# Causal attention prologue: another order of the features, of the stores and of the second batch's projections

## The chip, the cores and the metric

One core of one Trainium2 chip runs the whole program. The metric is the device time of one execution in microseconds; the kernel before took 1536.09 us, the median of three runs (1533.88 to 1536.41).

## What is computed

The program is a two-layer decoder on x of shape (2, 1024, 256), float32. Each step is added to x: linear attention with a feed-forward part, cross attention to a context of 64 rows, a recurrence, then in the second layer causal attention, context attention and a mixture of experts. The change is in the second layer's causal attention:

```python
h = layernorm(x)                            # (2, 1024, 256)
q, k, v = split(h @ Wqkv + bqkv)            # 16 heads of 16 features
score = einsum('bhsd,bhtd->bhst', q, k)     # keys after the query are masked out
attn = softmax(score / sqrt(16))
x = x + einsum('bhst,bhtd->bhsd', attn, v).reshape(2, 1024, 256) @ Wout + bout
```

## The kernel before

Everything is kept transposed, features on partitions and tokens on the free axis. Five engines run programs of their own, written out by hand and held together by semaphores; SP issues all DMAs. The layer is `causal_attention_layer`, L1761 to L2401.

**Three-part products.** q and k are float32, but their products are made in bfloat16: each of the two is split into three bfloat16 parts (the value, the rest, the rest of the rest), and six products of parts are stacked on the contraction axis. A stack is six times 16 rows, so 96 partitions; `Q_PART` and `K_PART` (L3641) say which part stands in which of the six places. Two more rows carry the negated maximum of each query, the "shift", against rows of ones in the key stack. Four heads (a "quad") lie side by side on the free axis: a stack is 98 partitions x 4 heads x 1024 tokens. There are four quads in a batch and two batches, so eight stacks of q and eight of k, kept in three buffers.

**How a stack is made.** ACT copies the projections of a batch out of PSUM with the bias (L2216) and casts parts 0 and 1 (L2235); DVE makes the rests and part 2 (L2291, L2293). Head h, feature d lies on row h*16+d. SP stores each part, 256 rows of 1024 tokens, to DRAM (`store`, L1926) in one DMA of 128 partitions and 512 KB, and loads it back in another shape (`load_part`, L1907): 16 partitions, the features, each with the four heads' rows of 2 KB one after the other. That is 12 DMAs of 128 KB for a quad: six for part 0, four for part 1, two for part 2. For the first batch SP's order is: store q0, k0, q1; wait for the part 0 stores; load part 0 of quad 0; store k1, q2, k2; wait for the part 1 stores, load part 1; wait for the part 2 stores, load part 2; then the second quad's 12 loads; then the first shift's rows (`keep_shift`, L1930) and the third quad's loads.

**What PE does meanwhile.** For batch 0 it projects q, k and v, then for batch 1 all of q, all of k and two of four groups of v (L2037 to L2059). Then come the first pieces. A "piece" is one PSUM tile of scores, query on the partition, made only to take its maximum per query on DVE (`reduce`, L2300). The first half of a quad's queries has eleven pieces (`NPC_0`). When they are reduced, DVE makes the negated maximum in two bfloat16 parts (`split_shift`, L2307, its operations at L2317 and L2319), PE transposes it (`turn_shift`, L2081), DVE copies it (L2326), SP moves its rows into the query stack (L1934), and only then PE can make the real scores (`scores`, L2088), ACT their exponentials (L2255), POOL the diagonal mask (L1998) and PE the values (`values`, L2104). The last two groups of v of batch 1 stand between the first pieces (L2161 to L2167). From there on PE alternates scores, pieces of later halves and values as `count_pieces` says.

**What POOL does meanwhile.** After its constants it waits until all six stores of the first batch have landed (L1977), because it writes the second batch's parts over the same tensors: a cast and a subtraction for each part, four operations for q and four for k (L1982 to L1988), and a memset of ones (L1991). Then it begins with the masks.

Of the kernel before, what the change touches and what calls it, by code (L numbers as in the profile page):

```python
# [28 lines left out]
P = 128  # L29
B, S, D = 2, 1024, 256  # L30
# [1730 lines left out]
def causal_attention_layer(nc, c):  # L1761

    H, DH = 16, 16
# [3 lines left out]
    HALVES = 2 * STEPS  # L1767
    ROWS, SHIFT = len(Q_PART) * DH, 2
    LOADS = 2 * len(Q_PART) * 16
    PAD = 32  # L1770
    RING = 16
    SCORES, TILES = 3, 4
# [56 lines left out]
    upto = count_pieces()  # L1829
# [18 lines left out]
    with ExitStack() as ctx:  # L1848
        bn, yn = c.bn, c.yn
        pr = c.signals(nc, "bp", dict(q_proj=4, k_proj=4, v_proj=4, q_raw=4, k_raw=4, v_copied=4))  # L1850
        s = c.signals(nc, "b", dict(part=0, rest=0, last_part=0, stored0=0, stored1=0, stored2=0, later_part=0, later_stored=0, ones=0, masks=0, k_ones=0,
                                       loaded0=0, loaded1=0, loaded2=0, shifted0=0, shifted1=0, made=0, read=0,
                                       max_step=0, parts=0, scored=0, expd=0, masked=0, av=0, out_copied=0, inv=0))
        set_round(0, s, pr)
# [47 lines left out]
        with nc.Block() as block:  # L1902

            @block.sync
            def _(sync):
                def load_part(n, i):

                    b, quad = divmod(n, QUADS)
                    a = n % 3
                    by_head = lambda ap: ap.rearrange("(h d) n -> d h n", d=DH)  # L1910
                    rows = slice(quad * QUAD * DH, (quad + 1) * QUAD * DH)
                    for r in range(len(Q_PART)):
                        if Q_PART[r] == i:
                            sync.dma_start(qs[a][r * DH:(r + 1) * DH], by_head(q_dram[b, i, rows, :])).then_inc(loaded[a].sem, 16)
                        if K_PART[r] == i:
                            sync.dma_start(ks[a][r * DH:(r + 1) * DH], by_head(k_dram[b, i, rows, :])).then_inc(loaded[a].sem, 16)

                def loads(n):
                    if n == 2:
                        sync.wait_ge(*pr["v_proj"](8))  # L1920
                    if n >= 3:
                        sync.wait_ge(*s["scored"](tiles_upto(first_group(2 * (n - 2)) - 1)))
                    for i in range(3):
                        load_part(n, i)

                def store(b, n, i, done):  # L1926
                    dram, parts = ((q_dram, q_parts), (k_dram, k_parts))[n]
                    sync.dma_start(dram[b, i].rearrange("(m p) n -> p m n", p=P), parts[:, i, :, :]).then_inc(done.sem, 16)

                def keep_shift(hs):  # L1930
                    _, _, half = part_of(hs)
                    sync.wait_ge(*s["read"](nth["shift", hs] + 1))
                    for i in range(SHIFT):
                        sync.dma_start(qs[hs // 2 % 3][ROWS + i:ROWS + i + 1, :, half * CH:(half + 1) * CH],  # L1934
                                       stage[i * QUAD:(i + 1) * QUAD, hs % 2, :]).then_inc(shifted[hs % 2].sem, 16)

                for n in range(2):
                    sync.wait_ge(*s["part"](n + 1))
                    store(0, n, 0, stored[0])
                sync.wait_ge(*s["part"](3))  # L1940
                store(0, 0, 1, stored[1])
                sync.wait_ge(*stored[0](2 * 16))
                load_part(0, 0)
                sync.wait_ge(*s["part"](4))
                store(0, 1, 1, stored[1])
                for n in range(2):
                    sync.wait_ge(*s["last_part"](n + 1))
                    store(0, n, 2, stored[2])
                for i in (1, 2):
                    sync.wait_ge(*stored[i](2 * 16))  # L1950
                    load_part(0, i)
                loads(1)
                keep_shift(0)
                loads(2)
                for hs in range(1, HALVES):
                    keep_shift(hs)
                    if hs == 3:
                        for n in range(2):
                            sync.wait_ge(*s["later_part"](4 * (n + 1)))
                            for i in range(3):  # L1960
                                store(1, n, i, s["later_stored"])
                    if hs % 2 == 1 and 3 <= hs // 2 + 2 < STEPS:
                        if hs // 2 + 2 == QUADS:
                            sync.wait_ge(*s["later_stored"](6 * 16))
                        loads(hs // 2 + 2)

            @block.gpsimd
            def _(pool):
# [7 lines left out]
                pool.memset(k_stack[ROWS:ROWS + SHIFT, :, :, :], 1.0).then_inc(s["k_ones"].sem)  # L1976
                for done in stored:  # L1977
                    pool.wait_ge(*done(2 * 16))
                pool.wait_ge(*s["k_ones"](1))
                for n, (raw, parts, ready) in enumerate(((raw_of[1][0], q_parts, pr["q_raw"]), (raw_of[1][1], k_parts, pr["k_raw"]))):  # L1980
                    pool.wait_ge(*ready(8))
# [35 lines left out]
            def _(pe):  # L2017
# [34 lines left out]
                for n in range(4):  # L2052
                    pe.wait_ge(*pr["k_raw"](n + 1))
                    project_in(1, "b_wq", n, c.bank(4 + n), pr["q_proj"])
                for n in range(4):
                    pe.wait_ge(*pr["v_copied"](n + 1))
                    project_in(1, "b_wk", n, c.bank(n), pr["k_proj"])
                later_value(0)
                later_value(1)  # L2059

                def tile(what):
                    n = nth[what]
# [41 lines left out]
                def values(pair):  # L2104
                    hs, first_ki = groups[2 * pair]
                    b, quad, half = part_of(hs)
                    pe.wait_ge(*s["expd"](tiles_upto(2 * pair + 1)))
                    if first_ki >= 4 * half:
                        pe.wait_ge(*s["masked"](diagonal_upto(2 * pair + 1)))
                    if first_ki == 0 and hs >= 1:  # L2110
                        pe.wait_ge(*s["out_copied"](hs))
                    for i in range(2):
                        ki, n = first_ki + i, width(first_ki + i, half)
                        for h in range(QUAD):
                            mm = pe.matmul(out_tile[h * PAD:(h + 1) * PAD, CH - n:CH], v_aug[:, b * TT + ki, quad * QUAD + h, :],  # L2115
                                           probs[(QUAD * (2 * pair + i) + h) % RING][:, 0:n],
                                           start=(ki == 0), stop=(ki == 4 * half + 3))
                    mm.then_inc(s["av"].sem)
# [36 lines left out]
                def more_pieces(first, last):  # L2155
                    for p in range(first, last):
                        piece(p)
                        if turned_after(p) is not None:
                            turn_shift(turned_after(p))

                pe.wait_ge(*s["masks"](2))  # L2161
                pe.wait_ge(*pr["q_raw"](8))
                more_pieces(0, 4)
                later_value(2)
                more_pieces(4, 8)
                later_value(3)
                more_pieces(8, upto[0])  # L2167
                pe.wait_ge(*s["k_ones"](1))
                pe.wait_ge(*pr["v_copied"](8))
                for slot in range(QUAD * len(groups)):  # L2170
                    (hs, ki), x = groups[slot // QUAD], slot % QUAD
                    if (slot // QUAD, x) in tile_at:
# [1594 lines left out]
```

## Time and profile before

| | us |
|---|---|
| median of three runs | 1536.09 |
| lowest, highest | 1533.88, 1536.41 |
| profiled execution | 1545.4 |
| its span | 1543.6 |
| PE busy | 1452.9 |
| DVE busy | 986.8 |
| ACT busy | 753.1 |
| POOL busy | 494.0 |

All times inside the program are counted from the start of the profiled execution's span. PE, DVE, ACT and POOL are the engines' busy times; SP is the engine that issues DMAs. The profiled execution is one run of its own; its 1545.4 us are 1.8 above its span and 9.3 above the median. The causal layer's projections begin at about 637 us, the first piece at 683.64, the first scores at 699.90.

### The profile page before, as it was taken

To read this page: it belongs to the slowest core of one execution; us is meant where nothing else is said; L and a number is where in the kernel's file an instruction comes from. 1 tells how busy PE (TensorE), PEld (TensorE's weight loads), DVE (VectorE), ACT (ScalarE), POOL (GpSimd) and SP (SyncE) were. 2 spreads that over 40 slices of the span, in tenths; PEclk is the share of its full clock that TensorE was granted. 3 is DMA by queue.
4 is the path that set the end of the run, shared out by engine and by line. 5 is a ranking of instruction groups with operands and counts; after the bars stand their busy time and mean duration, and the time that the engine had idled before them with its cause. 6 is when DMAs were issued, how large, how long until landed. Compare 5 with 4: busy or idle time off the path is not lost. (4 is left out here: it accounts for less than half of the span.)

```text
span 1543.6 us, 19029 instructions
## 1 busy us (share of the span) xinstructions
PE 1452.9 (94%) x6910; PEld 848.3 (55%) x6914; DVE 986.8 (64%) x1506; ACT 753.1 (49%) x1237; POOL 494.0 (32%) x410
## 2 busy tenths in 40 slices
PE   6999999989999999888999998898889999999998
PEld 3757764432232265453444443322568888888886
DVE  5774243768877743548888783676677575664853
ACT  5466344443334451543666565434655545445442
POOL 0046420123132410343111112102136655655562
PEclk9999997999999999998999999899999999999999
DMA  7000000000000000083535300000313223223201
GB/s 293 1 0 0 1 1 4 0 1 1 0 1 1 1 0 0 1 164 42 125 51 74 42 3 1 4 1 4 133 42 110 69 83 100 78 74 104 73 10 55
DMA packets 39044, 67.55 MB, mean 44 GB/s; under 512 B 3944, under 2 KB 19368, under 8 KB 38568
## 3 DMA queue, kind: packets, MB, share of 16 engines
q1 hardware_dynamic: 38952, 66.33, 16.1%
q8 instruction: 56, 0.92, 0.3%
q14 instruction: 36, 0.29, 0.1%
HBM read 57.80 MB, written 8.39 MB: 43 GB/s over the span
## 5 line engine op out<-in xcount | busy, mean ns | idle before, releaser
L2255 ACT ACTIVATE arena<-psum 128x512 f32<-128x512 f32 (+1 forms) x304 | 155.2, 583 | 109.9 <-PE psum L2100 109.2
L2303 DVE TENSOR_REDUCE b_mx<-psum 128x1 f32<-128x512 f32 (+3 forms) x304 | 179.6, 650 | 45.0 <-PE psum L2078 36.9
L3047 POOL TENSOR_TENSOR m_w_rest<-m_w,m_w_high 128x512 fp32r<-128x512 f32 (+1 forms) x88 | 111.6, 1270 | 155.6 <-ACT m_w_high L3246 155.6
L3497 DVE TENSOR_TENSOR m_hidden<-m_gelu,psum 128x512 f32<-128x512 f32 (+1 forms) x88 | 60.4, 686 | 148.6 <-ACT m_gelu L3338 124.4
L3140 PE MATMUL psum<-m_x_high,m_w_high 128*128 128x512 f32 (+1 forms) x352 | 138.4, 393 | 3.2 <-issue 3.2
L3053 POOL TENSOR_TENSOR m_h_rest<-m_hidden,m_h_high 128x512 fp32r<-128x512 f32 (+1 forms) x88 | 122.4, 1390 | 58.9 <-ACT m_h_high L3260 58.9
L3140 PE MATMUL psum<-m_x_rest,m_w_high 128*128 128x512 f32 (+1 forms) x352 | 138.0, 392 | 0.0
L3140 PE MATMUL psum<-m_x_high,m_w_rest 128*128 128x512 f32 (+1 forms) x352 | 138.0, 392 | 0.0
L3338 ACT ACTIVATE m_gelu<-psum 128x512 f32<-128x512 f32 (+1 forms) x88 | 52.5, 596 | 120.7 <-PE psum L3140 120.6
L1998 POOL TENSOR_SCALAR_AFFINE_SELECT arena<-arena 128x512 f32<-128x512 f32 x64 | 40.1, 637 | 212.7 <-ACT arena L2255 212.7
L1359 ACT ACTIVATE x_probs<-psum 128x1024 f32<-128x1024 f32 x56 | 57.3, 1024 | 90.9 <-PE psum L1097 90.9
L1517 DVE TENSOR_REDUCE x_mx<-psum 128x2 f32<-128x1024 f32 x64 | 76.6, 1217 | 35.5 <-PE psum L1071 35.3
L3260 ACT ACTIVATE m_h_high<-m_hidden 128x512 fp32r<-128x512 f32 (+1 forms) x88 | 55.7, 633 | 82.6 <-DVE m_hidden L3497 82.6
L2075 PE MATMUL psum<-b_k_stack,b_q_stack 96*128 96x512 bf16 (+3 forms) x288 | 88.2, 339 | 4.0 <-DVE b_mx L2303 1.9
L2100 PE MATMUL psum<-b_q_stack,b_k_stack 98*128 98x512 bf16 (+3 forms) x288 | 83.0, 332 | 4.4 <-DMA b_q_stack<-b_stage 3.1
L3140 PEld LDWEIGHTS psum<-m_x_high,m_w_high 128*128 128x128 f32 (+1 forms) x352 | 65.7, 187 | 18.5 <-issue 3.6
L3140 PEld LDWEIGHTS psum<-m_x_rest,m_w_high 128*128 128x128 f32 (+1 forms) x352 | 65.7, 187 | 15.1
L3140 PEld LDWEIGHTS psum<-m_x_high,m_w_rest 128*128 128x128 f32 (+1 forms) x352 | 65.6, 186 | 15.2
L3153 PE MATMUL psum<-m_h_high,m_o_high 128*128 128x512 f32 (+1 forms) x176 | 72.3, 411 | 0.2 <-POOL m_h_rest L3053 0.2
L2115 PE MATMUL psum<-arena,weights_sb 128*32 128x512 f32 (+3 forms) x768 | 71.7, 492 | 0.0
L1001 POOL TENSOR_TENSOR x_pool_sum<-x_probs 128x1024 f32<-128x1024 f32 x8 | 18.8, 2354 | 161.4 <-ACT x_probs L1359 161.4
L3153 PE MATMUL psum<-m_h_high,m_o_rest 128*128 128x512 f32 (+1 forms) x176 | 68.8, 391 | 0.0
(591 smaller groups left out, 3238.6 us busy)
## 6 DMA issues: line engine op xcount, KB each, us to landing
m_w<-w SPq DMA_DIRECT2D x32, 512.0 KB, 4.6
m_wo<-wo SPq DMA_DIRECT2D x16, 512.0 KB, 4.0
weights_sb<-weights SPq DMA_DIRECT2D x2, 2820.0 KB, 12.2
m_w<-w SPq DMA_DIRECT2D x16, 344.0 KB, 4.7
b_q_stack<-b_q_dram SPq DMA_DIRECT2D x36, 128.0 KB, 5.9
b_k_stack<-b_k_dram SPq DMA_DIRECT2D x36, 128.0 KB, 6.0
weights_sb<-weights SPq DMA_DIRECT2D x1, 3328.0 KB, 14.0
b_q_dram<-b_q_parts SPq DMA_DIRECT2D x6, 512.0 KB, 3.4
```

The costliest lines, as they stand in the source:

```text
L1359: ins = act.activation(probs[slot % RING][:], two_heads(units), ACT.Exp, scale=SCALE)
L1517: dve.tensor_reduce(mx[:, n % 2, i // 2, i % 2, :], two_heads(tile(("piece", n, i))), AX, ALU.max).then_inc(s["read"].sem)
L2075: mm = pe.matmul(bank[:, x * keys:(x + 1) * keys], qs[n % 3][0:ROWS, h, qi * P:(qi + 1) * P], ks[n % 3][0:ROWS, h, first:first + keys], st ...
L2100: mm = pe.matmul(score(i)[:, x * n:(x + 1) * n], ks[a][0:ROWS + SHIFT, h, ki * P:(ki + 1) * P], qs[a][0:ROWS + SHIFT, h, q0:q0 + n], start ...
L2115: mm = pe.matmul(out_tile[h * PAD:(h + 1) * PAD, CH - n:CH], v_aug[:, b * TT + ki, quad * QUAD + h, :], probs[(QUAD * (2 * pair + i) + h) ...
L2255: act.activation(quad_of(g)[:, heads[0]:heads[-1] + 1, 0:n], score(i)[:, 0:len(heads) * n].rearrange("p (h n) -> p h n", n=n), ACT.Exp, sc ...
L2303: dve.tensor_reduce(mx[:, part, qi, heads[0]:heads[0] + nh], tile(("piece", p))[:, 0:nh * keys].rearrange("p (h n) -> p h n", n=keys), AX, ...
L3047: pool.tensor_tensor(w_rest[:, n % W_RING, :, :, 0:H_N(n % HT)], raw_of(n), w_high[:, n % W_RING, :, :, 0:H_N(n % HT)].bitcast(F32), ALU.s ...
L3053: pool.tensor_tensor(h_rest[rows, n % H_RING, :], hidden[rows, n % 2, :], h_high[rows, n % H_RING, :].bitcast(F32), ALU.subtract).then_inc ...
L3140: mm = pe.matmul(c.bank(base + n % 2)[0:H_N(h), :], of[:, k, :], x_of[ex % 2][:, k, :], start=(k == 0 and i == 0), stop=(k == FT - 1 and i ...
L3153: mm = pe.matmul(total(m), of[rows, n % O_RING, m * P:(m + 1) * P], h_of[rows, n % H_RING, :], start=(h == 0 and i == 0), stop=(h == HT - ...
L3497: dve.tensor_tensor(hidden[rows, n % 2, :], gelu[rows, n % 2, :], c.bank(2 + n % 2)[rows, :], ALU.mult)\
```

## The change

Five things are changed together.

1. The host permutes the columns of the q and k projections (and their biases) inside each quad, so that row d*4+h holds head h, feature d. In DRAM the four heads' rows of one feature are then neighbours, and a load takes 16 rows of 8 KB in place of 64 rows of 2 KB. Destination and bytes are the same.
2. For the first batch each part's store is cut: the first quad's 64 rows (128 KB) are stored where the whole was stored, and the other rows in two DMAs (64 rows of the first half, 128 rows of the second) later: part 0 of q right after the two first stores, all others after quad 0's loads. SP waits for all twelve of these before it issues the second quad's loads.
3. POOL waits for the twelve too before it overwrites the parts.
4. PE makes only two of the four key projections of batch 1 before the first pieces; the other two and the first two groups of v stand between pieces, and the last two groups of v come after the twelfth piece and the shift's transpose.
5. PE waits for seven copied groups of v before the scores, and for the eighth before the first values.

```diff
@@ load_part @@
-                    by_head = lambda ap: ap.rearrange("(h d) n -> d h n", d=DH)
-                    rows = slice(quad * QUAD * DH, (quad + 1) * QUAD * DH)
+                    of_quad = lambda dram: dram[b, i, quad * QUAD * DH:(quad + 1) * QUAD * DH, :].rearrange("(d h) n -> d (h n)", d=DH)
+                    rows = lambda stack, r: stack[r * DH:(r + 1) * DH].rearrange("d h n -> d (h n)")
                     for r in range(len(Q_PART)):
                         if Q_PART[r] == i:
-                            sync.dma_start(qs[a][r * DH:(r + 1) * DH], by_head(q_dram[b, i, rows, :])).then_inc(loaded[a].sem, 16)
+                            sync.dma_start(rows(qs[a], r), of_quad(q_dram)).then_inc(loaded[a].sem, 16)
...
+                def store_first_quad(n, i):
+                    dram, parts = ((q_dram, q_parts), (k_dram, k_parts))[n]
+                    sync.dma_start(dram[0, i, 0:QUAD * DH, :], parts[0:QUAD * DH, i, 0, :]).then_inc(stored[i].sem, 16)
+
+                def store_others(n, i):
+                    dram, parts = ((q_dram, q_parts), (k_dram, k_parts))[n]
+                    sync.dma_start(dram[0, i, QUAD * DH:P, :], parts[QUAD * DH:P, i, 0, :]).then_inc(s["others_stored"].sem, 16)
+                    sync.dma_start(dram[0, i, P:D, :], parts[:, i, 1, :]).then_inc(s["others_stored"].sem, 16)
@@ SP's order @@
                 for n in range(2):
                     sync.wait_ge(*s["part"](n + 1))
-                    store(0, n, 0, stored[0])
+                    store_first_quad(n, 0)
+                store_others(0, 0)
                 sync.wait_ge(*s["part"](3))
-                store(0, 0, 1, stored[1])
+                store_first_quad(0, 1)
                 sync.wait_ge(*stored[0](2 * 16))
                 load_part(0, 0)
                 sync.wait_ge(*s["part"](4))
-                store(0, 1, 1, stored[1])
+                store_first_quad(1, 1)
                 for n in range(2):
                     sync.wait_ge(*s["last_part"](n + 1))
-                    store(0, n, 2, stored[2])
+                    store_first_quad(n, 2)
                 for i in (1, 2):
                     sync.wait_ge(*stored[i](2 * 16))
                     load_part(0, i)
+                store_others(1, 0)
+                for i in (1, 2):
+                    for n in range(2):
+                        store_others(n, i)
+                sync.wait_ge(*s["others_stored"](OTHERS * 16))
                 loads(1)
@@ POOL @@
                 for done in stored:
                     pool.wait_ge(*done(2 * 16))
+                pool.wait_ge(*s["others_stored"](OTHERS * 16))
@@ PE @@
-                for n in range(4):
+
+                def later_key(n):
                     pe.wait_ge(*pr["v_copied"](n + 1))
                     project_in(1, "b_wk", n, c.bank(n), pr["k_proj"])
-                later_value(0)
-                later_value(1)
...
+                later_key(0)
+                later_key(1)
                 pe.wait_ge(*s["masks"](2))
                 pe.wait_ge(*pr["q_raw"](8))
-                more_pieces(0, 4)
+                more_pieces(0, 2)
+                later_key(2)
+                more_pieces(2, 4)
+                later_key(3)
+                more_pieces(4, 6)
+                later_value(0)
+                more_pieces(6, NPC_0)
+                later_value(1)
+                more_pieces(NPC_0, upto[0])
                 later_value(2)
-                more_pieces(4, 8)
                 later_value(3)
-                more_pieces(8, upto[0])
                 pe.wait_ge(*s["k_ones"](1))
-                pe.wait_ge(*pr["v_copied"](8))
+                pe.wait_ge(*pr["v_copied"](7))
@@ host @@
+    by_quad = lambda m: m.reshape(-1, 4, QUAD, 16).transpose(0, 1, 3, 2).reshape(m.shape)
-        "b_wq": part(0), "b_wk": part(1), "b_wv": part(2), "b_wo": a["L1_attn_Wout"],
+        "b_wq": by_quad(part(0)), "b_wk": by_quad(part(1)), "b_wv": part(2), "b_wo": a["L1_attn_Wout"],
```

## Rows read from the trace of the kernel before

**Rows 1.** The page: span of the profiled execution and busy time by engine

```profile
span 1543.6 us, 19029 instructions
...
PE 1452.9 (94%) x6910; PEld 848.3 (55%) x6914; DVE 986.8 (64%) x1506; ACT 753.1 (49%) x1237; POOL 494.0 (32%) x410
```

**Rows 2.** Timeline of PE in the prologue: start us, us, engine, line, operation, operands, count

```profile
664.62 13.90 PE L2023 MATMUL psum<-weights_sb 128*128 128x512 f32 x32
678.36 3.62 PE L2029 MATMUL psum<-weights_sb 128*128 128x256 f32 x16
683.64 0.22 PE L2075 MATMUL psum<-b_k_stack,b_q_stack 96*128 96x128 bf16 x1 [1.67 <-DMA b_q_stack<-b_q_dram]
...
685.01 1.94 PE L2029 MATMUL psum<-weights_sb 128*128 128x256 f32 x8
...
690.35 0.38 PE L2075 MATMUL psum<-b_k_stack,b_q_stack 96*128 96x512 bf16 x1
696.17 0.59 PE L2085 MATMUL psum<-ident,b_shift 128*8 128x128 bf16 x4 [5.44 <-DVE b_shift L2319]
699.90 0.58 PE L2100 MATMUL psum<-b_q_stack,b_k_stack 98*128 98x512 bf16 x1 [3.14 <-DMA b_q_stack<-b_stage]
...
721.42 1.71 PE L2115 MATMUL psum<-arena,weights_sb 128*32 128x512 f32 x16
```

**Rows 3.** Timeline of DVE in the prologue, same columns

```profile
691.92 3.90 DVE L2317 TENSOR_SCALAR b_shift<-b_mx 128x16 bf16<-128x16 f32 x1
...
700.94 1.89 DVE L2303 TENSOR_REDUCE b_mx<-psum 128x1 f32<-128x512 f32 x3 [3.74 <-PE psum L2075]
703.08 13.31 DVE L2303 TENSOR_REDUCE b_mx<-psum 128x4 f32<-128x512 f32 x23 [0.25 <-PE psum L2078]
```

**Rows 4.** Timeline of POOL in the prologue, same columns

```profile
677.67 1.89 POOL L1982 CAST b_q_parts<-weights_sb 128x2048 bf16<-128x2048 f32 x1 [25.64 <-DMA b_k_dram<-b_k_parts]
...
691.73 4.06 POOL L1984 TENSOR_TENSOR arena<-arena,b_k_parts 128x2048 f32<-128x2048 f32 x1
...
706.75 0.64 POOL L1998 TENSOR_SCALAR_AFFINE_SELECT arena<-arena 128x512 f32<-128x512 f32 x1 [1.27 <-ACT arena L2255]
```

**Rows 5.** Timeline of SP, which issues the DMAs, same columns

```profile
660.43 0.39 SPq L1928 DMA_DIRECT2D b_q_dram<-b_q_parts  x1
662.23 0.38 SPq L1928 DMA_DIRECT2D b_k_dram<-b_k_parts  x1
664.70 0.36 SPq L1928 DMA_DIRECT2D b_q_dram<-b_q_parts  x1
...
669.36 0.63 SPq L1928 DMA_DIRECT2D b_k_dram<-b_k_parts  x1
674.73 0.32 SPq L1916 DMA_DIRECT2D b_k_stack<-b_k_dram  x1
...
697.23 1.41 SPq L1934 DMA_DIRECT2D b_q_stack<-b_stage  x2
```

**Rows 6.** Stretches: us, busy time of five engines, PEclk, DMA share, GB/s

```profile
681.00:691.00 10.00, 8.06 (x54) 5.90 (x52) 5.44 (x10) 1.79 (x3) 9.86 (x4) 1.00 1.09 142
751.00:755.00 4.00, 4.00 (x34) 1.72 (x27) 3.21 (x8) 2.21 (x5) 0.53 (x1) 1.00 1.05 400
```

**Rows 7.** DMA of the stretch 1293 to 1299 us: loads of expert weights, packets and 40 slices

```profile
GB/s 55 55 123 177 355 314 382 396 382 382 328 410 382 410 382 423 369 396 341 300 164 82 55 27 14 0 0 0 0 0 0 0 0 0 0 0 0 0 0 0
DMA packets 523, 1.01 MB, mean 168 GB/s; under 512 B 32, under 2 KB 32, under 8 KB 523
```

**Rows 8.** DMA rate in 40 slices of the stretch 679 to 691 us

```profile
GB/s 143 116 109 102 130 137 164 157 150 157 150 164 137 130 109 116 109 150 137 164 150 157 164 143 157 164 137 171 157 157 143 123 109 116 109 143 150 150 123 109
```

**Rows 9.** DMA issues of L1928, the stores: time to landing

```profile
DMA to landing us min/median/max: 2.7/5.7/8.1
```

**Rows 10.** Stretches around the pauses of PE, columns as in Rows 6

```profile
684.00:700.00 16.00, 7.42 (x51) 5.45 (x49) 11.40 (x15) 1.20 (x2) 15.70 (x6) 0.83 0.61 82
700.00:705.00 5.00, 5.00 (x19) 2.26 (x19) 3.81 (x7) 1.41 (x3) 4.94 (x2) 0.51 1.08 150
```

More of the change, by code:

```diff
@@ L1769, in causal_attention_layer @@
     LOADS = 2 * len(Q_PART) * 16
+    OTHERS = 2 * 3 * 2
     PAD = 32
@@ L1850, in causal_attention_layer @@
         pr = c.signals(nc, "bp", dict(q_proj=4, k_proj=4, v_proj=4, q_raw=4, k_raw=4, v_copied=4))
-        s = c.signals(nc, "b", dict(part=0, rest=0, last_part=0, stored0=0, stored1=0, stored2=0, later_part=0, later_stored=0, ones=0, masks=0, k_ones=0,
+        s = c.signals(nc, "b", dict(part=0, rest=0, last_part=0, stored0=0, stored1=0, stored2=0, others_stored=0, later_part=0, later_stored=0, ones=0, masks=0, k_ones=0,
                                        loaded0=0, loaded1=0, loaded2=0, shifted0=0, shifted1=0, made=0, read=0,
@@ L1909, in load_part @@
                     a = n % 3
-                    by_head = lambda ap: ap.rearrange("(h d) n -> d h n", d=DH)
-                    rows = slice(quad * QUAD * DH, (quad + 1) * QUAD * DH)
+                    of_quad = lambda dram: dram[b, i, quad * QUAD * DH:(quad + 1) * QUAD * DH, :].rearrange("(d h) n -> d (h n)", d=DH)
+                    rows = lambda stack, r: stack[r * DH:(r + 1) * DH].rearrange("d h n -> d (h n)")
                     for r in range(len(Q_PART)):
                         if Q_PART[r] == i:
-                            sync.dma_start(qs[a][r * DH:(r + 1) * DH], by_head(q_dram[b, i, rows, :])).then_inc(loaded[a].sem, 16)
+                            sync.dma_start(rows(qs[a], r), of_quad(q_dram)).then_inc(loaded[a].sem, 16)
                         if K_PART[r] == i:
-                            sync.dma_start(ks[a][r * DH:(r + 1) * DH], by_head(k_dram[b, i, rows, :])).then_inc(loaded[a].sem, 16)
+                            sync.dma_start(rows(ks[a], r), of_quad(k_dram)).then_inc(loaded[a].sem, 16)
                 def loads(n):
@@ L2107, in values @@
                     pe.wait_ge(*s["expd"](tiles_upto(2 * pair + 1)))
+                    if pair == 0:
+                        pe.wait_ge(*pr["v_copied"](8))
                     if first_ki >= 4 * half:
@@ L3738 @@
         "f_c0": a["L0_ffn_in_c"],
-        "b_bq": bias(0), "b_bk": bias(1), "b_bv": bias(2), "b_bo": a["L1_attn_bout"],
+        "b_bq": by_quad(bias(0)), "b_bk": by_quad(bias(1)), "b_bv": bias(2), "b_bo": a["L1_attn_bout"],
         "y_bq": a["L1_xattn_bq"], "y_bk": a["L1_xattn_bk"], "y_bv": a["L1_xattn_bv"], "y_bo": a["L1_xattn_bo"],
```

## The prediction

> **What bounds the kernel now.** The page first: over a span of 1543.6 us PE is busy 1452.9 us [rows 1], so only work of PE or a pause of PE can move the end; everything else is cover. The change lies in one place, the prologue of the causal layer, so I read PE's timeline there [rows 2] and look for pauses. There are three: 1.67 us before the first piece (683.64), released by a load of the query stack; 5.44 us before the transpose of the first shift (696.17), released by DVE; 3.14 us before the first scores (699.90), released by the DMA of the shift's rows. From 721.42, the first values, PE runs on nearly without a gap, so what counts is by how much that steady part moves.
>
> The middle pause is not what its label says. DVE finished the first half's eleven maxima at 691.9, and L2317, 16 elements per partition, then took 3.90 us [rows 3]. POOL started a 4.06 us subtraction at 691.73 [rows 4]; the two end within 0.04 us of each other. DVE's small operation stood still behind POOL's. The Trainium skill (SBUF — State Buffer, Who interferes with whom) says that DVE in a two-port mode and GpSimd exclude each other for a whole instruction; this pair agrees. POOL's chain of splits (L1982 to L1991) began at 677.67, released by the last stores, and ended at 705.48, 1.27 us before its first mask at 706.75: 27.8 us.
>
> Last, SP. It stores the three parts of q and k as the copies come (660.43, 662.23, 664.70, the last at 669.36), loads part 0 from 665.1, and begins the other loads at 674.73, when the part 1 stores landed [rows 5]. It issues the shift's two DMAs at 697.23; the scores start 2.67 us later.
>
> **What a load costs.** While only 16-partition loads run, the DMAs are saturated (share 1.09) at 142 GB/s; with the 128-partition stores they move 400 [rows 6]. One load is 128 KB, so 0.92 us; a 512 KB store is 1.31 us. The question of the change is whether 8 KB rows raise the 142. Both have 2 KB rows before, so the row length cannot be what separates 142 from 400. The loads of expert weights into 128 partitions run at 380 to 420 GB/s with a mean packet of 1.9 KB [rows 7], so the direction isn't it either. What is left is the number of partitions: 16 against 128, and that is not changed. Bounds for the new load: 142 GB/s (0.92 us) and 400 (0.33). I take 0.92, the row that has its partitions. Below it the slices of a pure load stretch go down to 102 GB/s and up to 171 [rows 8].
>
> The Trainium skill (SBUF — State Buffer, Door 1: The DMA port swizzle) says the same more sharply: partitions 0 to 15 reach four of 16 ports, measured at 104 GB/s for 1 MiB. By it the new loads would not gain, and with 104 a load would be 1.26 us.
>
> **The change, part by part,** in the span's clock. A store issued is moving 0.75 us later and has landed 0.65 us after its last byte (2.7 us at the least for a whole one [rows 9], less 1.31). That split is my estimate. Check on before: part 0 loads to 672.3, three stores of 1.31 to 676.2, six loads to 681.7; PE started at 683.64, so a load's tail is 1.9 us.
>
> *Stores cut to the first four heads.* 64 partitions x 2 KB, 128 KB. No row shows 64 partitions; bounds 0.33 us (400 GB/s) and 0.92 (142). I take 0.66, half the rate for half the partitions. Part 0's six loads move from 666.1 to 671.6, since their issue (after 664.70) does not change. Then three small stores end at 673.6. The first of them lands at 673.0, so SP issues the next loads there instead of at 674.73: six loads, 673.75 to 679.3, plus tail: **first piece at 681.2, 2.4 us earlier than 683.64.**
>
> *Keys 2, 3 and the values moved behind first pieces.* PE does one projection in 13.90 / 8 = 1.72 us and one value group in 1.78 (685.01 to 686.79). It starts the second batch at 664.6; four queries and two keys take it to 674.9, and it now idles 6.3 us to 681.2 instead of 1.67. Up to the eleventh piece it then has two keys (3.44), one value (1.78) and the pieces (3.1): 8.4 us; before it was 6.8. It also runs at the low clock: after the pauses of 5.44 and 3.14 us, 700 to 705 were granted 0.51, that is 1.2 GHz of 2.4 [rows 10]; the same 5 us or so here add 2.75 us. The last five maxima are DVE's (13.31 / 23 = 0.58 each, with a first wait): the eleventh is done 13 us after the first piece, at 694.2 (bounds 691.2 without the clock, 695 with a later start). Before: 691.9. So this part loses 2.3 us; the keys cost nothing of their own only while the loads are late, and they are not late enough.
>
> *POOL later.* Ten stores of the other heads (two DMAs per call, five calls) now follow the last load: issued from 675.9 at about 0.45 each (0.32 to 0.63 in [rows 5]), moving 679.3 to 685.9 (5 x 1.31), landed 686.5 (684.9 if 64 partitions go at the full rate). POOL starts then instead of at 677.67: casts and subtractions at 686.5 to 688.4, to 692.6, to 694.5, to 698.7. L2317 at 694.2 meets a cast and is through at 694.6; half a microsecond later it would meet a subtraction and wait until 698.7. Averaged over a pair, 1.7 us: transpose of the shift at about 695.9 (694.8 to 699.0) against 696.17. Values 2 and 3 (3.56) now fill PE while the shift's rows travel: PE is ready at 700.1 (699.0 to 703.2). POOL's chain ends at 714.3, the second mask at 715.7; the first values need it at 721.4, so 5 us of cover remain.
>
> *Second quad's loads later.* SP used to issue these 12 right behind part 2's; now it waits for all other stores, 686.5, and they move 687.3 to 698.3. The shift's rows, issued at about 697, stand behind them and land at 700.2 (2.67 less 0.75 after the queue is free). The loads themselves are needed only near 715. SP's third-quad loads follow the shift as before.
>
> *Sum.* Scores at 701.2 (700.2 to 703.2) against 699.90: +1.3. PE had only a short pause before them, so the low clock of 700 to 705 goes; DVE then shows gaps of 3.74 and 0.25 us and 13.31 us without one [rows 3], so it bounds from 703.1 and at most about 0.7 us is to be had. Net **+0.6 us**. The profiled execution took 1545.4 us, 9.3 above the median of the three runs; it would become 1546.0, and the median 1536.09 becomes **1536.7**. Its own range is 1533.5 to 1539.5: full-rate stores and no clock loss give scores at 698 (-2.6 with the clock's 0.7), a subtraction met and loads a few per cent slower give 704 (+3.4).
>
> **Rivals.** *The rows pay* (faster). If 8 KB rows lift the loads to 400 GB/s they become issue-bound, part 0 ends at 668.8, all by 673.8, the first piece starts at 675.5 with PE just free and at full clock, POOL and the second quad start at 681, L2317 (685.6) meets POOL's subtraction until 687.1, and the scores start near 691.6: -8.3, and -0.7 for the clock: 1527.1. Against it stands that 2 KB rows already run at 400; for it only that no row shows 16 partitions with longer rows. At 200 GB/s it is about half of that.
>
> *The shift's rows behind the second quad* (slower). Queued data decide as soon as the 12 loads end after 698.3. If 8 KB rows break the interleaving of loads to different partitions, the load goes at the low slices, 113 GB/s, 1.16 us: first piece +2.9, second quad +5.8, shift lands at 706.0, +6.1 less 0.7: 1541.5. It passes 0.2% from 123 GB/s down.
>
> *The reordering itself pays* (slightly faster): with PE at full clock, L2317 meets a cast and the half stores run at 400; scores at 698.6, -2: 1534, still inside no change.
>
> **Chances.** Forecast with its own range, the third rival in it, 0.67; rows pay 0.20; slower rival 0.13. One measurement of this kernel tells 0.2%, 3.1 us, from no change. The forecast gives 0.57 same, 0.06 faster, 0.04 slower; with the two rivals: **faster 0.26, same 0.57, slower 0.17.** The range takes in the fast case nearly whole and most of the slow one: 1526.8 to 1541.
>
> **What would show it.** DMA rate in loads-only stretches still near 142 GB/s though packets are 8 KB (at 300 or more the first rival holds). First piece at 681 after a pause of 6 us with a low clock behind it; L2317 later than 694, with a length set by POOL; POOL's first cast at 686.5, eight or nine us later; SP's second-quad loads from 686.5; the scores released by the DMA of the shift's rows or directly after the last values, near 701. The forecast is wrong if the scores start before 697 or after 704, or if the first values wait for a mask.

## The result, and the profile after

The changed kernel took 1542.71 us (median of 4 runs, 1541.38 to 1545.82) against 1534.99 for the kernel before on the same chip: a ratio of 1.0046, 95% interval 1.0034 to 1.0058. A second comparison (e5 below) gave 1543.01 against 1535.93, 1.0053 (1.0035 to 1.0071). It is slower by 7 us. The forecast was 1536.7, the range ended at 1541.0.

The two profiles seem to say the reverse. The page of the changed kernel:

```profile
span 1539.6 us, 19047 instructions
...
PE 1444.8 (94%) x6914; PEld 844.2 (55%) x6914; DVE 989.7 (64%) x1506; ACT 752.6 (49%) x1237; POOL 493.3 (32%) x410
```

Its span is 4 us shorter than that of before [rows 1]. The difference lies outside the change. The causal stage's first matmul starts at 629.23 us here and at 637.57 in the profile of before; a second profile of the kernel before started it at 637.01, others of kernels with the same earlier stages between 627.1 and 632.4. The window 228 to 262 us, in the cross attention and recurrence, before and then after (columns as in [rows 6]):

```profile
228.00:262.00 34.00, 31.55 (x84) 15.79 (x84) 11.40 (x26) 10.59 (x19) 2.26 (x9) 0.75 0.02 5
```

```profile
228.00:262.00 34.00, 31.80 (x100) 16.17 (x100) 14.65 (x33) 14.12 (x24) 2.25 (x9) 0.95 0.02 5
```

The clock granted to PE was 0.75 there in one run and 0.95 in the other, though nothing ahead of that place differs between the two kernels. So I count from the stage's first matmul, "stage time" below, and write before as 637.57, after as 629.23. In stage time the rows of before read: first piece 46.1, transpose of the shift 58.6, first scores 62.3 [rows 2], first values 83.9. PE in the changed kernel:

```profile
673.41 0.26 PE L2091 MATMUL psum<-b_k_stack,b_q_stack 96*128 96x128 bf16 x1 [6.68 <-DMA b_q_stack<-b_q_dram]
...
692.11 0.59 PE L2101 MATMUL psum<-ident,b_shift 128*8 128x128 bf16 x4 [5.18 <-DVE b_shift L2345]
692.63 5.62 PE L2046 MATMUL psum<-weights_sb 128*128 128x256 f32 x16
698.08 0.38 PE L2116 MATMUL psum<-b_q_stack,b_k_stack 98*128 98x512 bf16 x1
...
719.69 2.03 PE L2133 MATMUL psum<-arena,weights_sb 128*32 128x512 f32 x16
```

First piece at 44.2 (1.9 earlier), transpose at 62.9 (4.3 later), first scores at 68.9 (6.5 later), first values at 90.5 (6.6 later). The next layer's first memset on POOL, which marks the end of this stage, comes at 338.5 before and 345.4 after. The loss is made between the first piece and the first scores, and is kept.

DVE and POOL there, answering to [rows 3] and [rows 4]:

```profile
683.87 2.95 DVE L2329 TENSOR_REDUCE b_mx<-psum 128x1 f32<-128x384 f32 x5 [1.21 <-PE psum L2094]
686.85 3.29 DVE L2343 TENSOR_SCALAR b_shift<-b_mx 128x16 bf16<-128x16 f32 x1
690.17 1.80 DVE L2345 SCALAR_TENSOR_TENSOR b_shift<-b_mx,b_shift 128x16 bf16<-128x16 f32 x1
```

```profile
677.97 1.89 POOL L1999 CAST b_q_parts<-weights_sb 128x2048 bf16<-128x2048 f32 x1 [34.28 <-DMA b_k_dram<-b_k_parts]
...
686.04 4.06 POOL L2005 TENSOR_TENSOR b_q_parts<-weights_sb,b_q_parts 128x2048 bf16<-128x2048 f32 x1
690.05 1.89 POOL L1999 CAST b_k_parts<-arena 128x2048 bf16<-128x2048 f32 x1
...
705.81 0.63 POOL L2015 TENSOR_SCALAR_AFFINE_SELECT arena<-arena 128x512 f32<-128x512 f32 x1
```

POOL began at stage time 48.7 in place of 40.1. The eleventh maximum was done at 57.6, in place of 54.4. L2343, the split's first operation, then took 3.29 us: it ended 0.04 us after the subtraction of 686.04 (4.06 us long). And L2345, the second, 0.17 us before, took 1.80: it ended with the cast of 690.05. DVE lost to POOL twice.

Before, the second operation was not held, though POOL had a cast behind the subtraction there too:

```profile
695.85 0.17 DVE L2319 SCALAR_TENSOR_TENSOR b_shift<-b_mx,b_shift 128x16 bf16<-128x16 f32 x1
695.85 1.93 POOL L1986 CAST b_k_parts<-arena 128x2048 bf16<-128x2048 f32 x1
```

The difference is in which subtraction was met. Before it was one whose following cast waits for it by a semaphore, and that cast started 0.06 us after its end. In the changed kernel it was the last operation on q (L2005); the cast of k behind it does not wait for it, and is recorded from 690.05, before the subtraction's end at 690.10. The profiles of e5 and e6 below met this same one and show 1.80 again; those of e1, e2, e4, e8, e9 and e12 met one of the other kind and show 0.17 or 0.18. It is not a rule without exception: in e10 a memset of POOL that does wait started at the same recorded time as DVE's operation (704.90) and held it.

SP, answering to [rows 5], and three stretches, the first with the last loads of the first quad, the second with the second quad's loads, the third with the last two value groups:

```profile
661.01 0.50 SPq L1933 DMA_DIRECT2D b_k_dram<-b_k_parts  x1
665.18 0.31 SPq L1917 DMA_DIRECT2D b_k_stack<-b_k_dram  x1
...
667.84 0.45 SPq L1937 DMA_DIRECT2D b_k_dram<-b_k_parts  x1
...
677.68 0.32 SPq L1915 DMA_DIRECT2D b_q_stack<-b_q_dram  x1
...
693.17 1.41 SPq L1944 DMA_DIRECT2D b_q_stack<-b_stage  x2
```

```profile
666.00:671.00 5.00, 0.73 (x2) 0.00 (x0) 0.00 (x0) 0.69 (x1) 0.00 (x0) 0.82 1.12 157
679.00:690.00 11.00, 7.93 (x39) 5.02 (x37) 8.28 (x10) 2.19 (x4) 10.77 (x4) 0.97 1.04 132
693.00:698.00 5.00, 5.00 (x16) 4.06 (x16) 0.15 (x1) 0.60 (x1) 4.94 (x2) 0.65 0.01 2
```

The last store of the first quad, part 2 of k, is issued at 661.01 and the loads follow at 665.18, stage time 36.0 (before 37.2); the other heads' stores at 667.84, the second quad's loads at 677.68, stage time 48.5. They ran at 132 GB/s; the short first stretch shows 157, inside the 102 to 171 that single slices had before [rows 8]. And the last two value groups (692.63, 5.62 us for 16 matmuls) ran at a mean clock of 0.65.

### The profile page after: what moved, and what is told of

Same layout as the page of the kernel before. It is cut to its first block and busy times, and to the rows that moved or that the text cites. A ratio compares the mean times of both kernels' runs of the same rounds, so it can differ in the third digit from the quotient of the medians.

```text
span 1539.6 us, 19047 instructions
## 1 busy us (share of the span) xinstructions
PE 1444.8 (94%) x6914; PEld 844.2 (55%) x6914; DVE 989.7 (64%) x1506; ACT 752.6 (49%) x1237; POOL 493.3 (32%) x410
## 5 line engine op out<-in xcount | busy, mean ns | idle before, releaser
L1359 ACT ACTIVATE x_probs<-psum 128x1024 f32<-128x1024 f32 x56 | 57.3, 1023 | 89.2 <-PE psum L1097 89.2
```

The lines of the kernel that those rows point to most:

```text
L1359: ins = act.activation(probs[slot % RING][:], two_heads(units), ACT.Exp, scale=SCALE)
```

## The experiments

All times that follow are stage times unless a row shows them. Ratios are to the kernel before, run on the same chip in turn. The table gathers what each kernel's profile showed; "next layer" is that first memset of the next layer. e12 was run once beside before and has no interval.

| kernel | first piece | split done | first scores | next layer | ratio (95%) |
|---|---|---|---|---|---|
| before | 46.1 | 58.4 | 62.3 | 338.5 | 1 |
| changed | 44.2 | 62.7 | 68.9 | 345.4 | 1.0046 (1.0034 to 1.0058) |
| e1 rows alone | 45.2 | 57.3 | 61.2 | 338.7 | 1.0004 (0.9986 to 1.0022) |
| e2 changed, old PE order | 43.0 | 55.0 | 63.6 | 339.8 | 1.0008 (0.9988 to 1.0028) |
| e3 changed, POOL aside | 43.0 | 56.3 | 61.8 | 337.2 | 1.0003 (0.9984 to 1.0023) |
| e4 before again | 46.5 | 58.6 | 62.4 | 338.6 | 0.9999 (0.9980 to 1.0018) |
| e5 changed again | 43.3 | 62.0 | 67.6 | 343.0 | 1.0053 (1.0035 to 1.0071) |
| e6 changed, values fill | 42.9 | 61.6 | 65.4 | 342.8 | 1.0026 (1.0009 to 1.0044) |
| e7 before, POOL aside | 45.2 | 53.8 | 57.5 | 333.7 | 0.9971 (0.9948 to 0.9993) |
| e8 PE order alone | 46.7 | 60.6 | 64.6 | 341.6 | 1.0023 (1.0006 to 1.0040) |
| e9 e2, shift first | 43.0 | 54.8 | 58.7 | 340.0 | 1.0001 (0.9982 to 1.0021) |
| e10 e9, POOL aside | 43.2 | 51.8 | 55.6 | 339.0 | 1.0000 (0.9982 to 1.0019) |
| e11 e7 again | 45.0 | 53.7 | 57.3 | 333.5 | 0.9974 (0.9956 to 0.9991) |
| e12 other order of loads | 44.9 | 57.3 | 61.2 | 338.9 | one run |

Up to the first scores e1, e12 and before do the same work but for the loads, and e4 is before itself: their 61.2 to 62.4 show how far the stage moves without a cause that I changed. The column "next layer" also holds short spells at the low clock late in the stage: in e1, e8, e9 and e12 a stretch of 50 us behind stage time 250 was granted 0.97, in before and the changed kernel 1.00, which is worth about 1.5 us.

**e1, the rows alone.** The kernel before with the host's permutation and the 8 KB rows, hunks `load_part` and host of the diff.

> The kernel before with the new feature order and 8 KB rows alone. My theory: a load is bound by its 16 partitions, not by its rows, so the loads-only stretches stay at 130 to 145 GB/s, the first piece starts 46 us after the stage's first matmul as before, and the time is that of before within 2 us. Rival (the rows pay): loads at 300 GB/s or more, first piece limited by PE, 4 us or more faster. Rival (the rows cost): below 120 GB/s and 2 us or more slower.

The stretch with the second quad's loads alone:

```profile
669.00:680.00 11.00, 9.01 (x58) 7.29 (x57) 4.43 (x8) 2.19 (x4) 10.77 (x5) 1.00 1.04 133
```

133 GB/s against 142 in [rows 6], and the same time within an interval of 2 us down and 3 us up. Four times longer rows bring nothing that can be seen. Neither rival holds: the rows are neither the gain nor the loss of 7 us.

**e2, PE's order of before, all else changed.**

```diff
-                def later_key(n):
+                for n in range(4):
                     pe.wait_ge(*pr["v_copied"](n + 1))
                     project_in(1, "b_wk", n, c.bank(n), pr["k_proj"])
+                later_value(0)
+                later_value(1)
...
-                more_pieces(0, 2)
-                later_key(2)
...
+                more_pieces(0, 4)
                 later_value(2)
+                more_pieces(4, 8)
                 later_value(3)
+                more_pieces(8, upto[0])
```

> The changed kernel with PE's order of before: all four keys and two value groups ahead of the first piece. Stores, loads and POOL as changed. My theory: the order on PE is what makes the maxima late and lets DVE's split meet two operations of POOL; without it the first piece starts about 44.4 us after the stage's first matmul, the maxima are done at 52.7, and the first scores come between 61 and 63.5, held by the shift's rows behind the second quad's loads: within 2 us of before, so 5 to 7 faster than the changed kernel. Rival (the stores and POOL's later start are the cost): it stays 5 us or more slower than before.

Same as before in time, as expected. PE's two waits and SP's two issues, the first of the second quad's loads and the shift's rows:

```profile
683.06 0.58 PE L2102 MATMUL psum<-ident,b_shift 128*8 128x128 bf16 x4 [5.04 <-DVE b_shift L2336]
691.53 0.59 PE L2117 MATMUL psum<-b_q_stack,b_k_stack 98*128 98x512 bf16 x1 [7.89 <-DMA b_q_stack<-b_stage]
```

```profile
676.36 0.32 SPq L1915 DMA_DIRECT2D b_q_stack<-b_q_dram  x1
...
684.12 1.41 SPq L1944 DMA_DIRECT2D b_q_stack<-b_stage  x2
```

The split's second operation still took 0.17 us, as before. The split was done at 55.0, 3.4 us earlier than before, but the shift's rows, issued at 684.12, let PE go 7.4 us later, where [rows 5] and [rows 2] show 2.7: they stood behind twelve loads that began at 676.36. What the earlier stores won was lost in that queue.

**e3, POOL stands aside in the changed kernel.** One wait:

```diff
                     pool.wait_ge(*s["later_part"](4 * n + 3))
+                    if n == 0:
+                        pool.wait_ge(*s["parts"](1))
```

> The changed kernel, with one wait added: POOL starts the last of its four operations on q only after DVE has split the first shift. My theory: DVE's two small operations, 3.29 and 1.80 us in the changed kernel, take 0.17 each; PE's pause of 5.2 us before the shift's transpose falls under 1.5 and with it the low clock behind it; first scores at about 62.8 us after the stage's first matmul in place of 68.85: 5 to 6.5 us faster than the changed kernel, within 2 of before. Rival (the maxima are late because of PE's order, POOL is only beside it): the transpose comes at most 2 us earlier and the gain is under 2.5 us.

DVE's split and PE's two waits:

```profile
685.63 0.17 DVE L2345 TENSOR_SCALAR b_shift<-b_mx 128x16 bf16<-128x16 f32 x1
685.84 0.17 DVE L2347 SCALAR_TENSOR_TENSOR b_shift<-b_mx,b_shift 128x16 bf16<-128x16 f32 x1
```

```profile
686.16 0.38 PE L2103 MATMUL psum<-ident,b_shift 128*8 128x128 bf16 x4 [0.44 <-DVE b_shift L2347]
...
691.49 0.38 PE L2118 MATMUL psum<-b_q_stack,b_k_stack 98*128 98x512 bf16 x1 [1.30 <-DMA b_q_stack<-b_stage]
```

3.29 and 1.80 us became 0.17 and 0.17, PE's pause before the transpose 0.44 in place of 5.18, the first scores came at 61.8 (expected 62.8), 7.1 us earlier than in the changed kernel's first profile and 5.9 earlier than in its second (e5), and the whole loss was gone. Not all of the 7.1 is POOL's hold: the maxima too were done earlier here, at 55.9 for 57.6 and 56.4. The rival, which gave POOL under 2.5 us, falls.

**e4, before again.** No edit.

> The kernel before once more, for a second profile. Theory: the profiled execution shown of it lost about 8 us to the low TensorE clock in the recurrence's stage and 2 later on, before and behind the place of the change; this one starts the stage nearer to 629 us than to 637 and takes about 1535. From the stage's first matmul to the first scores it takes 62.3 us again, within 1.5. Rival: the stage itself varies by as much as 5 us from run to run.

The first scores came within 0.1 us of before, although the maxima were done 2.1 us later (56.4 for 54.4): the split took 1.91 us in place of 3.90 and ended with the same subtraction of POOL, so the end of POOL's subtraction set the time. But this run too started the stage late, at 637.01, so the expected 629 was wrong, and its window 228 to 262 us was granted 0.75 again, where the others had 0.90 or 0.95. Why these two profiles had the lower clock stays open.

**e5, the changed kernel again.** No edit.

> The changed kernel once more, on the chip of the kernels sent with it. My theory: first scores 68.8 us after the stage's first matmul, within 1.5, because DVE's split of the shift meets a subtraction and then a cast of POOL; the causal stage ends 6 to 8 us later than before, and the time is 5 to 8 us above before, whatever the clock does in earlier stages. Rival (the 0.46% of the first comparison was the chips' spread, which is as wide among runs of before): under 3 us.

The split's operations took 3.76 and 1.80 us, the first scores came at 67.6, the next layer at 343.0, 4.5 us later than before; a little less than the 6 to 8 expected of the stage, while the time was 7.1 us above. The rival falls.

**e6, values in the pause.** The last two value groups ahead of the shift's transpose:

```diff
-                more_pieces(NPC_0, upto[0])
+                piece(NPC_0)
                 later_value(2)
                 later_value(3)
+                turn_shift(0)
```

> The changed kernel with the last two value groups moved ahead of the shift's transpose, into PE's pause of 5.2 us; POOL and DVE as they are. My theory: the pause is not the loss, DVE's two blocked operations are; the transpose stays at 62.9 us after the stage's first matmul, the first scores come when the shift's rows land, at 66.6 in place of 68.85: 2 us faster than the changed kernel and still 4 us or more slower than before. Rival (PE's order and low clock are the whole loss): within 2 us of before.

```profile
690.44 0.58 PE L2101 MATMUL psum<-ident,b_shift 128*8 128x128 bf16 x4 [2.39 <-DVE b_shift L2346]
694.16 0.59 PE L2116 MATMUL psum<-b_q_stack,b_k_stack 98*128 98x512 bf16 x1 [3.14 <-DMA b_q_stack<-b_stage]
```

The transpose stayed (61.7), the scores waited for the shift's rows instead of for the values: 65.4, 3.4 us earlier than changed (2.2 from e5), and the ratio halved to 1.0026. So at the first scores the position of the values, slow at the low clock, is a term of its own of about 2 us, and DVE's wait is the larger one. How much of it lasts is less sure: the medians of e6 and e5 are 3.0 us apart, but their intervals overlap, and the next layer began at 342.8 and 343.0.

**e7, POOL stands aside in the kernel before.** The same wait ahead of the first subtraction on k (`4 * n + 1`, `n == 1`).

> The kernel before, with one wait added: POOL starts its first subtraction on k only after DVE has split the first shift. My theory: the 3.65 to 3.90 us that this split takes before become 0.17, the first scores come at 58.8 us after the stage's first matmul in place of 62.3, and the kernel is 2.5 to 4.5 us faster than before. Rival (the second quad's loads or POOL's later masks take it up): under 1.5 us.

```profile
680.60 0.18 DVE L2319 TENSOR_SCALAR b_shift<-b_mx 128x16 bf16<-128x16 f32 x1
680.80 0.17 DVE L2321 SCALAR_TENSOR_TENSOR b_shift<-b_mx,b_shift 128x16 bf16<-128x16 f32 x1
```

```profile
681.12 0.38 PE L2087 MATMUL psum<-ident,b_shift 128*8 128x128 bf16 x4 [1.72 <-DVE b_shift L2321]
684.65 0.59 PE L2102 MATMUL psum<-b_q_stack,b_k_stack 98*128 98x512 bf16 x1 [3.14 <-DMA b_q_stack<-b_stage]
```

The first scores came at 57.5, 4.8 us earlier than before; PE's pause is 1.72 in place of 5.44. 1528.69 us against 1535.93: 4.5 us by the ratio (1.1 to 8.0), 7.2 by the medians. This beats both kernels. Of the 4.8 us about 1 is the stage's own movement: against e1 and e12, whose maxima were done as early (53.5 and 53.2), the first scores gained 3.7.

**e8, PE's order alone.** The PE hunks of the diff on the kernel before.

> The kernel before with PE's new order alone; rows, stores, loads and POOL's start as before. My theory: the first piece starts at 46 us after the stage's first matmul as before, the maxima are done at 58 to 60 in place of 54.35, and the first scores come 4 to 8 us later than before, by which of POOL's operations the split meets: 4 to 8 us slower. Rival (the order costs nothing unless POOL starts late as well): within 2 us of before.

```profile
688.33 1.38 DVE L2326 TENSOR_SCALAR b_shift<-b_mx 128x16 bf16<-128x16 f32 x1
689.75 0.17 DVE L2328 SCALAR_TENSOR_TENSOR b_shift<-b_mx,b_shift 128x16 bf16<-128x16 f32 x1
```

The split began at 59.0, 4.7 us later than before, as the order alone makes it, but it met POOL only for 1.38 us. Here POOL itself had been held: its k operations began at 54.3 and not at 52.2, since ACT's last key copy was late. The first scores came 2.3 us later than before and the time was 1.0023, 3.5 us, both under the expected 4 to 8. The interval, 0.9 to 6.1 us, excludes no cost at all, but not the rival's 2 us.

**e9, shift's rows first.** e2's kernel with two lines of SP exchanged, `keep_shift(0)` ahead of `loads(1)`.

> The kernel of e2 (changed kernel, PE's order of before) with SP issuing the first shift's rows ahead of the second quad's 12 loads. My theory: in e2 the rows were issued at 56.2 us after the stage's first matmul and let PE go only at 63.6 because they stood behind the loads; now it is 2.7 us, so the first scores come at 58.9 and the kernel is 2.5 to 5 us faster than before. Rival (the 7.4 us are the price of something else in the DMA, or the loads are then late for the second quad's pieces): first scores at 62 or later, or the gain gone by the first values.

```profile
687.10 0.58 PE L2117 MATMUL psum<-b_q_stack,b_k_stack 98*128 98x512 bf16 x1 [3.20 <-DMA b_q_stack<-b_stage]
```

The rows let PE go 2.7 us after their issue, the first scores came at 58.7 as expected; yet the time was that of before. PE later, at the first values:

```profile
710.36 3.22 PE L2132 MATMUL psum<-arena,weights_sb 128*32 128x512 f32 x16
```

1.71 us in [rows 2], 3.22 here. A second spell at the low clock, which began at stage time 74 before, fell on the values here (granted 0.50 from 708 to 712 us). Ahead of it POOL's memset, later than before, had held the second half's split for 0.7 us (0.90 in place of 0.17). By the second quad's first transpose only 0.3 us of 3.6 were left, and the late spell named under the table took these. The expected gain was missed; the rival's last words, the gain gone by the first values, come nearest, though 1.8 us of it were still there then.

**e10, both in one.** e9 with POOL's wait before its second operation on q.

> The kernel of e9 with POOL standing aside for DVE's split, here before its second operation on q. My theory: split at 51.5, first scores at 55.4; but POOL's chain, 8.6 us late from the stores, ends near 78, and the second mask near 79 holds the first values, which would otherwise be ready at 77; so of the 3.4 us gained over e9 about 2 are left, 5 to 7 us faster than before and within 2 of e7. Rival (POOL's later chain costs nothing here): 8 us or more faster than before.

The first scores came at 55.6 as expected. DVE and POOL behind them:

```profile
702.73 2.15 DVE L2333 TENSOR_TENSOR b_mx<-b_mx 128x16 f32<-128x16 f32 x1
704.90 3.53 DVE L2336 TENSOR_SCALAR b_shift<-b_mx 128x16 bf16<-128x16 f32 x1
708.47 0.18 DVE L2338 SCALAR_TENSOR_TENSOR b_shift<-b_mx,b_shift 128x16 bf16<-128x16 f32 x1
```

```profile
700.78 4.06 POOL L2007 TENSOR_TENSOR b_k_parts<-arena,b_k_parts 128x2048 bf16<-128x2048 f32 x1
704.90 3.51 POOL L2010 MEMSET weights_sb<- 2x4096 bf16 x1
```

Not the mask held the first values, as I had written, but the second half's split: 2.15 and 3.53 us behind POOL's late subtraction and memset, against 0.18 and 0.90 in e9, and 0.18 and 0.17 before. (L2333 joins the two partial maxima of that half, L2336 and L2338 are the split.) PE waited 6.2 us. Of 6.7 us won at the first scores 1.4 were left at that half's transpose, and the low clock behind the wait took the rest by the second quad's first transpose. POOL's later start costs a second time.

**e11, e7 again.**

> The kernel of e7 once more, beside e9 and e10 on one chip. Theory: 6 to 8 us faster than before again, first scores at 57.5 to 59. Rival (its first result was luck of the clock, since the scores came only 4.8 us earlier): 3 us or less.

0.9974 (0.9956 to 0.9991), first scores at 57.3: 4.0 us by the ratio, 5 by the medians, 1531.30 against 1536.38, less than the 6 to 8 expected. The interval (1.4 to 6.8 us) leaves no room for "no gain" but some for the rival's 3. The stage itself repeats within 0.2 us (333.5).

**e12, the loads in another order.** In the kernel before, `load_part` of the second and later quads replaced by a loop over an order written out: `q0 q1 q4 q5 q2 q3 k4 k5 k0 k1 k2 k3` for odd quads, `q0 k0 q2 k2 q1 k1 q3 k3 q4 k4 q5 k5` for even ones, the digit being the block of 16 partitions.

> The kernel before with the 12 loads of the second and later quads issued in another order, the same bytes to the same places: for quads 1, 3, 5, 7 neighbouring loads go to blocks of 16 partitions whose ports differ by the Trainium skill's map (0-15, 16-31, 64-79, 80-95, 32-47, 48-63 and so on), for quads 2, 4, 6 up to four in a row go to blocks that share theirs. Theory (a load is bound by the few ports that its 16 partitions reach): quad 2, 4, 6 load at 100 to 120 GB/s, 13 us or more for 1.5 MB, quads 1, 3, 5, 7 at 150 or more, 10.5 us or less. Rival (the bound is something else that 16 partitions bring, the same for all): both at 130 to 145 GB/s, 11 to 12 us. The time itself within 2 us of before, since these loads are hidden.

Loads-only stretches of quads 2, 4, 5 and 7, then quad 2 in the kernel before:

```profile
691.00:701.00 10.00, 8.73 (x41) 3.46 (x40) 9.75 (x17) 2.93 (x6) 5.09 (x3) 0.84 1.09 112
770.00:781.00 11.00, 11.00 (x87) 5.21 (x86) 10.17 (x20) 8.01 (x17) 0.87 (x2) 1.00 1.08 121
800.00:810.00 10.00, 10.00 (x81) 4.79 (x73) 9.21 (x18) 7.64 (x16) 0.17 (x1) 1.00 1.07 129
868.00:877.00 9.00, 9.00 (x74) 4.10 (x66) 8.20 (x16) 6.70 (x14) 0.11 (x1) 1.00 1.07 141
```

```profile
701.00:711.00 10.00, 8.93 (x42) 3.68 (x40) 9.75 (x17) 2.89 (x6) 5.06 (x3) 0.81 1.08 128
```

112 and 121 GB/s in the even quads shown, where before had 128 for quad 2 and 139 for quad 4; 129 and 141 in the odd ones, where before had 130 and 131. The order matters by some 12% where neighbours share ports, and spreading them gives nearly nothing over before. Neither theory's numbers hold in full: 150 is not reached. Fixed windows cut such loads at different places; taken over the middle 80% of each quad's bytes, quads 2, 4 and 6 ran at 117, 122 and 126 GB/s here and at 126 to 138, 132 to 150 and 131 to 138 in the profiles of before, e4, e7, e8 and e11, which have the order of before. So the slower even quads are more than the spread. What is shown, in one profile, is that the rate depends on the order of the loads; that it is the partitions and not the alternation of q and k, which the even order also has, was not tested. The Trainium skill (SBUF — State Buffer, Door 1: The DMA port swizzle) gives partitions 0 to 15 four ports and 104 GB/s for 1 MiB. All rates here lie above that, and the nearest is the order in which neighbours share ports; that fits ports as the bound, but the runs do not prove it. One run (1534.55 beside 1534.08) gives no sign that the loads are not hidden.

## Why the prediction was wrong

*The rows.* Right. 133 and 132 GB/s were measured for 142 taken.

*The first piece.* Expected 2.4 us earlier, came 1.9 earlier: the loads of part 1 were issued at 36.0, where I had 35.4. The pause before it (6.68 us) and the low clock behind it came as worked out.

*The maxima.* Expected done at 694.2, stage time 56.6; came at 57.6.

*POOL's start.* Expected 8.8 us later, came 8.6 later.

*The sum at the split.* This is where it failed. I took POOL's hold as an average over its operations, 1.7 us, and the worst case as one subtraction met. In the runs of the changed kernel DVE met a subtraction, 3.3 to 3.8 us, and then its second operation, two inputs from SBUF, met the cast behind it, another 1.6 us. Together 4.8 us were lost where I had 1.7. The clash is not random: the stage repeats within 1 to 2 us from run to run, so a mean over phases was the wrong way to price it. And the prediction has no term for the second operation, which had cost nothing before. The transpose came at 62.9, where the forecast had 58.3 and my worst case 61.4; 1.0 of this are the maxima.

*The values behind the transpose.* I had written that the pause would shrink, so that PE would be at full clock for the last two value groups (3.56 us). With the split late the pause stayed, 5.18 us, the clock behind it was 0.65, and they took 5.45 to the scores. That is another 1.9 us. The terms came together: scores 6.5 us late against 1.3 forecast and 3.3 at the worst, outside the 697 to 704 that I had named as the sign of being wrong (704 is stage time 66.4, they came at 68.9).

*The sum itself.* It has two slips, neither of which decides anything. PE ready at 700.1 and the rows landed at 700.2 give scores at 700.2, not the 701.2 that the sum uses; nothing in it stands for the other 1.0 us. And the transpose was put at the end of the hold, 695.9, though before it started 0.35 us behind the end of L2317.

*The shift's rows in the queue.* Right as a mechanism, as e2 shows (7.4 us for 2.7), but in the changed kernel the split was later than the queue, so it decided nothing. The slower rival named this queue, at a lower rate of loads; that rate never came. The slower end came by another cause.

*The mask.* POOL's chain ended 0.1 us before its first mask, in place of 1.27, and the first values did not wait; but in e10 it was POOL's late chain that took everything back, through DVE and not through the mask.

What the 7 us need is shown: taking POOL out of the way removes them all (e3), and so does the old PE order (e2). PE's order alone gives about half (e8, 3.5 with an interval of 0.9 to 6.1), so the rest comes from its meeting POOL's later start. What stays open is the exact size of the parts: the changed kernel's two profiles end the stage 4.5 and 6.9 us later than before, the medians are 7.1 and 7.7 apart, and how much of this the clock adds, here and in other stages, was not separated.

## What to carry to other kernels

Before a long chain on GpSimd is moved, look for small VectorE operations on the critical path that it can hold, and give GpSimd a wait so that it steps aside: one semaphore wait won 4.0 to 4.5 us here (ratios of e11 and e7). A clash that repeats in every run must be priced at the phase where it falls, with each following operation, and not at its mean. A transfer that the critical path waits for belongs ahead of bulk loads in the same queue (2.7 us in place of 7.4). But a gain at one point of a prologue should be followed to the steady part before it is believed: here that one was gone by the second quad (e9).

## What the runs showed that I had not expected

VectorE's tensor_scalar of 16 elements per partition, from SBUF in float32 to bfloat16, was held 3.53 us by a GpSimd memset that reads nothing (704.90 to 708.41, e10), not only by operations that read. The Trainium skill (SBUF — State Buffer, Who interferes with whom) says that a VectorE operation in a two-port mode and GpSimd lock each other out for a whole instruction; the trace agrees. For a VectorE operation with two SBUF inputs it names only GpSimd instructions that read SBUF. The two that were held here, L2333 (2.15 us, e10) and the changed kernel's L2345 (1.80 us), stood behind a subtraction and a cast, which read, so this agrees too.

The place where the stage starts moved by 10 us between profiles of kernels with the same earlier stages (627.1 to 637.6), with the granted clock of one earlier stretch between 0.75 and 0.95. Two single profiles can therefore show the opposite sign of a difference of 7 us.
